# Loads for the output products behind the last head's stack, with their widenings, and the products one pair of rounds later

## The reference

```python
h = _layernorm(x, axis=-1) * (1 + ca) + sa
x = x + ga * attn(h)      # 16 heads of 32 channels, rope, causal softmax, then y @ Wo.T + bo
h = _layernorm(x, axis=-1) * (1 + cb) + sb
x = x + gb * experts(h)   # best 8 of 48 kept experts, up to 192 tokens each
```

## Time and profile before

| | |
|---|---|
| median of 3 runs | 4376.86 us (4376.18 to 4387.05) |
| the profiled execution | 4383.56 us |
| its span | 4381.8 us |
| TensorE busy | 3863.3 us, 88% |
| GpSimd busy | 2773.6 us, 63% |
| VectorE busy | 2732.0 us, 62% |
| ScalarE busy | 1803.8 us, 41% |
| chain that ended last | TensorE 60%, issue 14%, GpSimd 11%, DMA 6% |
| mean granted clock of TensorE | 0.939 of full speed |

### The profile page before, as it was taken

The page is one execution under the profiler, slowest core; times in us unless marked ns, Lnnn a source line. Parts: engine busy times, 40 slices in busy tenths (PEclk is TensorE's granted clock), DMA queues, the critical chain, the costliest instruction groups (busy, mean ns, idle before and its releaser), DMA issues.

```text
span 4381.8 us, 85215 instructions
## 1 busy us (share of the span) xinstructions
PE 3863.3 (88%) x21344; PEld 2343.0 (53%) x21344; DVE 2732.0 (62%) x5837; ACT 1803.8 (41%) x3526; POOL 2773.6 (63%) x2251
## 2 busy tenths in 40 slices
PE   2989999886989998877899998869899998859998
PEld 1755544455744554456654454447555444547776
DVE  2767677455757766465667775457676774546555
ACT  1335555422345555333355554323355554211111
POOL 2768788723768878615678888407587886315454
PEclk7989999997989999988899999979899998979999
DMA  5443333243433334234433333324433332449998
GB/s 193 160 136 81 97 97 105 79 146 105 172 111 95 81 98 122 69 142 134 162 89 95 98 97 103 135 83 160 140 79 97 96 104 79 146 124 257 259 249 194
DMA packets 305622, 555.81 MB, mean 127 GB/s; under 512 B 59892, under 2 KB 99956, under 8 KB 301812
## 3 DMA queue, kind: packets, MB, share of 16 engines
q1 hardware_dynamic: 283640, 491.91, 37.6%
q0 software_dynamic: 21504, 58.40, 5.7%
HBM read 318.15 MB, written 174.85 MB: 113 GB/s over the span
## 4 chain that ended last, share of the span: by engine, by line
PE 60%; issue 14%; POOL 11%; DMA 6%; DVE 4%; ACT 2%; SPq 2%; DVEq 0%; POOLq 0%; ACTq 0%
PE PS L1293 16%; PE PS L1269 12%; PE PS L1246 12%; PE PS L1190 5%; PE PS L1390 4%; POOL qs L951 3%; POOL t L948 3%; PE PS L1401 2%; DMA out<-z,it 2%; POOL Sm L974 2%; DMA QK<-qkd 2%; POOL hTl L926 2%; PE PS L1327 2%; PE PS L1272 1%; SPq L681 1%
## 5 line engine op out<-in xcount | busy, mean ns | idle before, releaser
L1091 ACT ACTIVATE Pt<-PS 128x512 f32<-128x512 f32 (+3 forms) x2560 | 1204.3, 543 | 1069.7 <-PE PS L1269 613.0
L974 POOL TENSOR_TENSOR Sm<-Pt 128x512 f32<-128x512 f32 (+3 forms) x960 | 1028.3, 1077 | 451.7 <-ACT Pt L1091 448.9
L1570 DVE TENSOR_REDUCE part<-PS 128x1 f32<-128x512 f32 x1536 | 1003.7, 685 | 350.1 <-PE PS L1246 342.9
L1246 PE MATMUL PS<-QK 96*128 96x512 f32 (+3 forms) x2560 | 1033.6, 422 | 125.1 <-DMA QK<-qkd 51.1
L1269 PE MATMUL PS<-QK 97*128 97x512 f32 (+3 forms) x2560 | 996.7, 410 | 42.3 <-DMA QK<-mT 21.0
L1293 PE MATMUL PS<-Pt,V 128*32 128x512 f32 (+3 forms) x5120 | 873.5, 555 | 19.4 <-POOL Sm L974 19.3
L1297 PE MATMUL PS<-Sm,onesv 128*32 128x512 f32 (+3 forms) x1920 | 822.0, 536 | 0.0
L1566 DVE CUSTOM_DVE_ANT_0 PS<-PS,consts 128x128 f32<-128x128 f32 (+3 forms) x1024 | 504.0, 495 | 454.8 <-PE PS L1246 449.3
L1269 PEld LDWEIGHTS PS<-QK 97*128 97x128 f32 x2560 | 491.1, 194 | 477.8 <-issue 349.8
L974 POOL TENSOR_TENSOR Sm<-Sm,Pt 128x512 f32<-128x512 f32 (+1 forms) x640 | 712.2, 1113 | 50.2
L1246 PEld LDWEIGHTS PS<-QK 96*128 96x128 f32 x2560 | 501.5, 197 | 333.8 <-DVE part L1570 107.2
(11 more groups left out here) (164 smaller groups left out, 4821.9 us busy)
## 6 DMA issues: line engine op xcount, KB each, us to landing
QK<-qkd SPq DMA_DIRECT2D x720, 128.0 KB, 3.1
qkd<-st SPq DMA_DIRECT2D x64, 1024.0 KB, 4.5
Wg<-wgu SPq DMA_DIRECT2D x48, 768.0 KB, 5.6
o<-od SPq DMA_DIRECT2D x448, 64.0 KB, 2.0
W<-wd SPq DMA_DIRECT2D x4, 6144.0 KB, 21.6
Wd<-wdn SPq DMA_DIRECT2D x48, 384.0 KB, 7.2
xin<-x SPq DMA_DIRECT2D x16, 1024.0 KB, 7.6
vd<-vst SPq DMA_DIRECT2D x16, 1024.0 KB, 6.1
```

Of the source, the lines that this page charges most:

```text
L974: nc.gpsimd.tensor_tensor(total, of[0][:, first:CH] if i == 1 else total, of[i][:, first:CH], ALU.add).then_inc(sum_done, 1)
L1091: nc.scalar.activation(Pt[:, t % NPT, first:CH], S2[t % NS2][:, first:CH], ACT.Exp, scale=SCALE).then_inc(exp_done, 1)
L1246: mm(s1[:, 0:w], QK[0:3 * HD, hh % 2, 0, qb * P:(qb + 1) * P], QK[0:3 * HD, hh % 2, 1, c * CH:c * CH + w], start=True, stop=True).then_inc ...
L1570: v.reduce_max(part[:, qb, cc:cc + 1], s1[:, 0:w], AX.X).then_inc(s1_dve, 1)
```

## The change

SP issues the loads `load_attention` and `load_tokens` of chunks 0 and 1 no longer at the end of pass `H - 2` of its loop, ahead of the stack of head 15, but in pass `H - 1`, behind that stack, the second maxima row of head 14, the move of head 13's last chunk and that of head 14's chunk 0. The widening of chunk 0 moves from the start of head 14 to behind the pair that ends with the first round of head 15, that of chunk 1 from the middle of head 14 to behind rounds 5 and 6 of head 15, ahead of the join of chunk 0. The products with Wo go from (one, two, two, two, one) behind the pairs from rounds 7 and 8 of head 15 on, to (two, two, two, two) behind the pairs from rounds 9 and 10 on; the last two then stand behind the last values. The products (0,0) and (0,1) then come behind the scaling of chunk 1 in the list.

```diff
--- before.py
+++ after.py
@@ -156,7 +156,7 @@
 LAST_CHUNK = sum(qb < NT - TPC for qb, _, _ in TILES) + 8
 TILES_FROM = 2
 FIRST_TILES_FROM = 4
-OUT_AT = (8, 9, 10, 11, 12, 13, 14, 16)
+OUT_AT = (10, 10, 11, 12, 13, 14, 15, 16)
 
 
 def stream():
@@ -199,8 +199,8 @@
             closing[last + t].append(("moments",))
     closing[last + NR].append(("normed",))
     closing[NR * (H - 3)].append(("fold",))
-    closing[NR * (H - 2) + 1].append(("widen", 0))
-    closing[NR * (H - 2) + 7].append(("widen", 1))
+    closing[last - 1].append(("widen", 0))
+    closing[last + 5].append(("widen", 1))
     out = []
     for n in range(0, NR * H + 12, 2):
         if n < NR * H:
@@ -780,6 +780,10 @@
                     if hh >= 2:
                         move(hh - 2, NCH - 1)
                     move(hh - 1, 0)
+                    if hh == H - 1:
+                        for j in range(2):
+                            load_attention(j)
+                            load_tokens(j)
                     if h == 0 and g == NG - 1:
                         output_weights()
                     at = b * T + (hh - 1) * P
@@ -792,10 +796,6 @@
                     if h == 1 and hh > 1:
                         store_group(g - 1, range(NCH - 1, NCH))
                     move(hh - 1, 2)
-                    if hh == H - 2:
-                        for j in range(2):
-                            load_attention(j)
-                            load_tokens(j)
                     if h == 1 and g + 1 < NG:
                         load_values(g + 1)
                     if h == 0 and g < NG:
```

## The result

The changed kernel takes 4329.22 us (median of 4 runs, 4326.68 to 4331.38), the kernel before 4381.95 (4 runs, 4376.18 to 4389.52). The ratio is 0.9878, with a 95% interval of 0.9859 to 0.9898. The forecast was 4326 us, range 4304 to 4346.

What follows compares the result with a forecast made beforehand. TensorE, busy 88% of the span, was taken as the bound, its idle time as what can be won. Stack wait -51, widening -5.3 and head 15 +5.2 us took the median 4376.86 to 4326 us, range 4304 to 4346.

Steps and rivals of the forecast that it cites:

- The first hole: Head 15's stack, late behind the loads: stretch between maxima-transpose marks falls from 24.81 to 11.65 us, 51 us over four batches.
- The widening out of head 14: Chunk 1's widening inside head 14 cost TensorE 1.33 us per batch; moving it out wins 5.3 us in all.
- The cover of what is behind the loads: Head 15's first maxima row behind the moved loads: 2.6 us to spare at worst, some 10 usually; priced at nothing.
- GpSimd in head 15: Both widenings among GpSimd's sums there: value(15,2) comes 1.8 us late, TensorE waits 4.3 us for round 7's sum.
- The walk: GpSimd's order in head 15, followed in the old time scale: gaps of 3.65 us, chunk 0's scaling ends at 872.3.
- The price of head 15: Products one pair later, with both widenings in head 15: +1.3 us per batch, +5.2 in all; bounds -6.6 and +9.1.
- the old hole: TensorE's 5.17 us stop ahead of the products with Wo; granted clock 0.69 in the 5 us behind it, assumed unchanged.
- The sum: All terms together: -51 - 5.3 + 5.2 = -51 us, giving 4326 us, 1.2% faster.
- the slow restart: Time lost to TensorE's lower clock after waiting: 2.7 us behind the stack wait, some 1.4 behind the wait before Wo.

## Why the prediction was right

*The first hole.* The stretch between marks (14,1) and (15,0) went to 11.62 us, forecast 11.65. What put the stack off is shown: the move of the loads without the rest is worth 47.6 us by difference, the widening in the hole has no part in it, and the delay is split into issuing and bytes. The forecast of 51 us for this step was 55.3 in the profiled execution. Of the 4.3 us more, 3.5 are batch 3 of before, which ran at the low clock for 15 us behind its wait (6.3 us on top of it, forecast 2.7).

*The widening out of head 14.* 23.59 us between marks, forecast 23.6.

*The cover of what is behind the loads.* Priced at nothing, and nothing was awaited. The loads went out at 808.55, 8.1 us ahead of the row (estimated 5 to 9), and the row at 816.67, forecast 815 on a scale that runs 1.45 us earlier. The experiment with the row behind the loads shows a delay of 10 us from issue to use, the figure that I took as the worst.

*GpSimd in head 15.* The walk gave waits of 1.8 and 4.3 us and the scaling 26.3 us behind mark (15,1); measured are 1.64, 4.54 and 26.21. The experiments have the wait ahead of the first product at 9.6 us with the products left in place, and at 0.4 with the widenings left in head 14 or put behind the scaling.

*The price of head 15.* Forecast +1.3 us per batch, measured +1.9 in batch 0 and 1.6 on average. The first product starts 26.97 us behind the mark instead of 26.4, because the two value rounds behind the wait run at the low clock to their end: the granted clock of the 5.3 us behind the wait is 0.54, where I had taken the 0.69 of the old hole.

*The sum.* -51 forecast, -52.7 by medians. The two mis-sizings, 4 us more at the hole and 1 us more in head 15, both concern the slow restart behind a wait. They have opposite signs, and the first hangs on how long the low clock lasted in one batch, which nothing in the prediction could tell: that the sum came within 2 us is in part luck.

## What to carry to other kernels

In a queue in order find the last urgent entry without slack, and put bulk loads behind it, counting both the time to issue them and their bytes. Here the loads ahead of one row of 4 KB instead of behind it gave the whole gain back. Work that is moved with the loads needs a hole of its own: walk the receiving engine's order with the durations of the trace, and look for its idle time behind the need, not only ahead of it; that was worth another 26 us.

## What the runs showed of the hardware beyond that

A VectorE add with both inputs in SBUF (128x2048, f32, 2.37 us) holds GpSimd's adds up for most of its length: 1.75 us of GpSimd's work took 5.58 beside two of them. They ran side by side from 830.80 to 835.26; 1.12 us of GpSimd's work was left then, so it had done some 0.6 us of it in 4.5 (an estimate from these rows). With adds of 128x512 the two engines share the time: VectorE's take about twice as long (9.21 us instead of 4.74), GpSimd's 10% to 70% longer. That this comes from where the inputs lie was not tested.

A wait of 3.7 us on TensorE cost 6.8 us and one of 10.4 us cost 13.2. The runs with a hole in head 14 have 24 such waits, of 3.2 to 11.6 us. In 22 of them the price beyond the wait's own length is 2.1 to 3.3 us, little dependent on that length; in the other two (waits of 10.02 and 3.63 us) it is 6.3. In the stretches read, TensorE is busy all through the restart, and the granted clock goes with the price: 0.50, 0.76 and 1.00 in three stretches of 5 us behind the usual wait of 10.44 us, and 0.50 in all three behind each of the two dear ones. How much of the price is the clock was not measured by itself.
